# A one-column carry copy in an attention kernel, issued by ScalarE instead of VectorE

## The reference, cut to what matters

```python
def _time_mix_layer(x, ln_w, ln_b, Wk, Wv, Wr, Wo):
    normed = _layer_norm(x, ln_w, ln_b)
    k = jnp.einsum('btd,ed->bte', normed, Wk)
    v = jnp.einsum('btd,ed->bte', normed, Wv)
    r = jax.nn.sigmoid(jnp.einsum('btd,ed->bte', normed, Wr))
    kv = k * v
    def step(state, kv_t):
        state = DECAY * state + (1.0 - DECAY) * kv_t
        return (state, state)
    _, states = jax.lax.scan(step, init, jnp.swapaxes(kv, 0, 1))
    y = r * jnp.swapaxes(states, 0, 1)
    return x + jnp.einsum('btd,ed->bte', y, Wo)
```

## Time and profile before

| | us |
|---|---|
| median of 3 runs | 1204.03 |
| lowest and highest of them | 1203.22, 1205.99 |
| span of the profiled execution, first to last instruction | 1212.0 |
| own time of the profiled execution | not given beside its span |
| busy in the span: PE, DVE, ACT, POOL | 1091.2, 909.5, 614.8, 652.6 |

### The profile page before, as it was taken

The page is one execution under the profiler, slowest core; times in us unless marked ns, Lnnn a source line. Parts: engine busy times, 40 slices in busy tenths (PEclk is TensorE's granted clock), DMA queues, the critical chain, the costliest instruction groups (busy, mean ns, idle before and its releaser), DMA issues. The chain is left out here.

```text
span 1212.0 us, 22064 instructions
## 1 busy us (share of the span) xinstructions
PE 1091.2 (90%) x6624; PEld 957.5 (79%) x6624; DVE 909.5 (75%) x2050; ACT 614.8 (51%) x1019; POOL 652.6 (54%) x560
## 2 busy tenths in 40 slices
PE   6999999999999998757999999999999999999900
PEld 6778887777777786646888888888888999999900
DVE  5788888888888887744776766777776778888737
ACT  3345444444444444333444555555555666666528
POOL 1011554444444544665667667666573777777534
PEclk9899999999999998859999999999999999999965
DMA  4011221111121121356566657878775888998569
GB/s 157 18 53 52 53 54 53 53 52 52 52 52 52 52 53 36 76 138 180 127 150 168 158 126 168 207 200 210 182 202 156 196 248 243 241 221 246 112 190 383
DMA packets 80243, 164.34 MB, mean 136 GB/s; under 512 B 27568, under 2 KB 44976, under 8 KB 79920
## 3 DMA queue, kind: packets, MB, share of 16 engines
q1 hardware_dynamic: 49968, 127.72, 33.4%
q0 software_dynamic: 30208, 35.81, 16.8%
HBM read 118.78 MB, written 44.70 MB: 135 GB/s over the span
## 5 line engine op out<-in xcount | busy, mean ns | idle before, releaser
L1181 POOL DMA_INDIRECT x_acc<-fy_sb,pair_out x136 | 254.2, 1869 | 133.8 <-issue 56.0
L1371 PE MATMUL fring<-fxh,fw_hi 128*128 128x256 f32 (+1 forms) x704 | 236.0, 335 | 11.7 <-issue 8.0
L1373 PE MATMUL fring<-fxh,fw_lo 128*128 128x256 f32 (+1 forms) x704 | 234.2, 333 | 0.0
L1372 PE MATMUL fring<-fxl,fw_hi 128*128 128x256 f32 (+1 forms) x704 | 233.9, 332 | 0.0
L1201 ACT ACTIVATE fw_hi<-w_raw 128x1024 fp32r<-128x1024 f32 x156 | 163.4, 1054 | 107.9 <-PE fy L1416 90.1
L1263 DVE TENSOR_TENSOR fw_lo<-w_raw,fw_hi 128x1024 fp32r<-128x1024 f32 x156 | 189.6, 1219 | 15.5 <-ACT fw_hi L1201 12.4
L98 POOL DMA_INDIRECT xg<-x_src,pair_in x136 | 147.9, 1088 | 85.2 <-issue 43.6
L546 POOL TENSOR_TENSOR rs<-ve,neg_half 128x4 f32<-128x4 f32 x48 | 55.6, 1159 | 254.6 <-DVE nm L633 254.5
L88 POOL DMA_INDIRECT slot_list<-pairs,slot_u x128 | 144.5, 1129 | 50.3 <-issue 35.6
L870 PE MATMUL ring<-xh,w_hi 128*128 128x512 f32 x384 | 160.7, 418 | 2.1 <-issue 2.0
L1414 PE MATMUL fy<-fw_hi,gh 128*128 128x256 f32 x544 | 155.8, 286 | 0.0
(11 more groups left out here) (149 smaller groups left out, 2013.1 us busy)
## 6 DMA issues: line engine op xcount, KB each, us to landing
w_raw<-w_ffn SPq DMA_DIRECT2D x156, 512.0 KB
x_in<-h SPq DMA_DIRECT2D x16, 512.0 KB
x_src<-x SPq DMA_DIRECT2D x16, 512.0 KB
x_acc<-x SPq DMA_DIRECT2D x16, 512.0 KB
acc<-x_acc SPq DMA_DIRECT2D x16, 512.0 KB, 7.1
out<-o SPq DMA_DIRECT2D x16, 512.0 KB, 6.2
xg<-x_src,pair_in POOLq DMA_INDIRECT x136
x_acc<-fy_sb,pair_out POOLq DMA_INDIRECT x136
```

Source lines behind the costliest of these rows:

```text
L1181: nc.gpsimd.indirect_dma_start(x_acc, bass.IndirectOffsetOnAxis(pair_out[j][:, q, 0:1].bitcast(U32), 0), y[j][:, q, :], None, compute_op=A ...
L1371: nc.tensor.matmul(out, hi, rows_hi, start=dc == 0, stop=False)
L1372: nc.tensor.matmul(out, hi, rows_lo, start=False, stop=False)
L1373: last = nc.tensor.matmul(out, lo, rows_hi, start=False, stop=dc == DC - 1)
```

## The change

The carry copy of `recur` leaves VectorE's stream. A new function of ScalarE, `carry_on`, does the same copy as an activation with function Copy. For layer 1 it is issued in front of `keep_k` of e=1 (for e=0) and behind `x_hi(1, s-1)` (for e=1); for layer 2 behind `keep_k` of e=1 (for e=0) and at the end of ScalarE's step (for e=1). It is left out for chunk 15. The scan now waits until the carry of the chunk before it, same e, has been copied, since `state` is overwritten.

```diff
+            def carry_on(l, n, e):
+
+                if within(n, 0, CHUNKS - 2):
+                    act.wait_ge(s_sn[l], n * 2 + e + 1)
+                    nc.scalar.activation(carry[:, l, e, bass.ds(n + B, 1)], state[l][:, e, CH - 1:CH],
+                                         ACT.Copy).then_inc(s_cy[l], 1)
+
...
                             normalize(1, xr, normed[1], s - 1, s_n[1])
+                        if e == 1:
+                            carry_on(0, s, 0)
                         if at(s, 0):
                             keep_k(0, s, e, j, None, 0)
...
                 if layer2:
                     x_hi(1, s - 1)
+                if layer1:
+                    carry_on(0, s, 1)
                 if at(s, CHUNKS):
                     normalize3(s, half, j)
...
                         keep_k(1, s - 1, 1, j, s_kv[0], s * 2 + 2)
+                    carry_on(1, s - 1, 0)
...
                 if layer2:
                     gate_r(1, s - 1, 1, j)
+                    carry_on(1, s - 1, 1)
...
                 if within(n, 1, CHUNKS):
                     dve.wait_ge(s_y[l], n * 2 + e - 1)
-                dve.wait_ge(s_cy[l], n * 2 + 2)
+                if within(n, 1, CHUNKS):
+                    dve.wait_ge(s_cy[l], n * 2 + e + 1)
+                else:
+                    dve.wait_ge(s_cy[l], 2)
                 nc.vector.tensor_tensor_scan(state[l][:, e, :], decay[:, :], kv[:, e, :],
                                              carry[:, l, e, bass.ds(n, 1)], ALU.mult, ALU.add).then_inc(s_sn[l], 1)
-                dve.wait_ge(s_sn[l], n * 2 + e + 1)
-                nc.vector.tensor_copy(carry[:, l, e, bass.ds(n + B, 1)], state[l][:, e, CH - 1:CH]).then_inc(s_cy[l], 1)
```

## The result

The changed kernel takes 1188.75 us (median of 4 runs, 1186.91 to 1190.67) against 1203.72 us (4 runs) before: 15.0 us less, a ratio of 0.9871, 95% interval 0.9845 to 0.9898. It is faster, as forecast, and by more: the forecast was 1192.5 and the range began at 1189.0, 0.25 us above what came.

A forecast was written before the change was run, and what follows sets the result against it. One 30.12 us loop through VectorE, GpSimd, ScalarE and TensorE, none full, was the bound. Step savings summed to 11.6 us, span 1212.0 to 1200.4, less 8.0 for the median: forecast 1192.5 us, range 1189 to 1199 (8 in 10).

The forecast's parts named there:

- ScalarE's price of 0.10: ScalarE's layer 1, e=0 copy between normalizing activations and keep_k: costs the loop 0.10 us per step, bounds 0 and 0.36.
- the second reading: Odd step before took 0.45 us longer through 0.44 us idle VectorE ahead of xr, so VectorE time returns one to one.
- start, to the gate copy of step 3: Attention's first steps: start and end together save 0 to 0.2 us.
- steps 3, 4, 14: Written-out attention steps: 0.47 us each from three copies of 0.19 less 0.10, taken as 1.2 us for TensorE's little waiting.
- steps 5, 13: Attention steps half in and half out of the loop: save 0.9 us each, 1.8 us together.
- even steps 6, 8, 10, 12: Even loop steps: each saves 0.36 + 0.41 + 0.30 - 0.10 = 0.97 us, 3.9 us together.
- odd steps 7, 9, 11: Odd loop steps, with the iteration's end: each saves 0.36 + 0.82 + 0.36 - 0.10 = 1.44 us, 4.3 us together.
- step 15: Attention step behind the written-out step 14: both layer-2 copies save 0.4 us.
- A: VectorE's issue time moves to the next instruction, each copy gives back only 0.19 us; 1198 us; chance 0.15.
- B: TensorE becomes the bound, or the later part gives some back; 1191 to 1196 us; chance 0.13 beyond the forecast's own bounds.
- C: Nothing arrives: some wait put down as slack binds in each step; 1203 to 1205 us; chance 0.05.
- D: Slower: ScalarE's copy ahead of keep_k costs over about 1.1 us per step, as with table loads (1206.6 us); chance 0.07.

The follow-up runs named there:

- wait_back: Changed kernel with VectorE again waiting for the scan's semaphore right behind each scan, without a copy of its own; median 1199.1 us, ratio to before 0.9959.
- defer: Kernel before, all four copies still on VectorE but each issued one or two operations later; median 1191.1 us, ratio to before 0.9901.
- before_again: Kernel before, unchanged, profiled once more; 1206.3 us (1 run), profile span 1204.4 us.
- unroll_before: Kernel before with all 20 steps written out, no hardware loop; median 1196.8 us, ratio to before 0.9880.
- after_again: Changed kernel, unchanged, timed and profiled again; median 1197.5 us, ratio to before 0.9892.
- unroll_after: Changed kernel with all 20 steps written out, no hardware loop; median 1186.2 us, ratio to before 0.9813.
- three: Changed kernel with the layer 1, e=0 copy put back on VectorE, the other three on ScalarE; median 1191.6 us, ratio to before 0.9913.
- act_twice: Changed kernel with one more one-column ScalarE activation in front of the layer 1, e=0 copy; median 1195.3 us, ratio to before 0.9860.

## Why the prediction was right and where it was not

**Right: the loop, the places and the mechanism.** The four engines are one loop; time off VectorE in it comes back one to one; three of four copies count; a copy costs much more than its 0.15 us. wait_back shows that the wait is what costs, defer that the engine hardly matters, the two written-out kernels that the iteration's end and the loop's addresses were part of it. ScalarE's price of 0.10 was 0.09. An even step was to save 0.97 and saves 0.91 (30.12 to 29.21). That is what its parts give: the gate copy to the end of the layer-2 statistics is 0.70 shorter in step 10, `kv` to `xl` 0.29 shorter, `normed` to `keep_k` 0.08 longer.
The Trainium skill ("ScalarE: Activation LUTs", Rules for kernel authors) has about 0.3 us for an activation whose bias is a pointer operand. The copy here has no bias, so that figure was not its price, though the prediction took it for every activation. The rows here give 0.20 from start to end and 0.09 from start to start.

**Right by luck: the second reading.** "Its one difference" between the odd and the even step before was said to be the 0.44 us ahead of `xr`, and that number met the 0.45 us between the steps. The rows say otherwise. The last operation of the layer-2 statistics (`nm`), and the activations that wait for it through GpSimd, in step 9 and in step 10:

```profile
301.93 0.16 DVE L633 TENSOR_SCALAR nm<-mv 128x4 f32<-128x4 f32 x1
305.02 2.08 ACT L407 ACTIVATE normed<-xr,nb,rs 128x256 f32<-128x256 f32 x4 [2.92 <-POOL nb L548]
...
332.30 0.16 DVE L633 TENSOR_SCALAR nm<-mv 128x4 f32<-128x4 f32 x1
335.21 2.08 ACT L407 ACTIVATE normed<-xr,nb,rs 128x256 f32<-128x256 f32 x4 [2.32 <-POOL nb L548]
```

From the gate copy to `nm` the odd step took 13.83 us and the even one 13.63, only 0.20 apart, since the even step has delays of its own (the 0.30 ahead of the scan at 321.98 among them). From `nm` to `normed`, GpSimd's part, it was 3.09 against 2.91, 0.18 apart. The remaining 0.07 lies behind. That is also why the steps did not come out alike, as the prediction wanted them, but the odd ones shorter: without the 0.44 the even step's own delays are left.

**Wrong: the size.** The mechanism was right, and what failed was the sum. It gave 11.6 us; the same terms came to 14.5 at step 18, by the differences of the two first profiles. The odd steps are the term that was too small by most (4.3 against 5.1), then the written-out steps, step 15 and the start:

| term of the sum | said | measured |
|---|---|---|
| start, to the gate copy of step 3 | 0 to 0.2 for start and end | 0.57 |
| steps 3, 4, 14 | 1.2 | 1.81 |
| steps 5, 13 | 1.8 | 1.99 |
| even steps 6, 8, 10, 12 | 3.9 | 3.71 |
| odd steps 7, 9, 11 | 4.3 | 5.10 |
| step 15 | 0.4 | 0.99 |
| step 16 | in "start and end" | 0.33 |

The start's 0.57 is 0.97 less 0.40: the first `kv` starts at 22.90 after and at 23.30 before, ahead of any carry, and before_again has it at 23.08, so that is scatter of the first loads. The 0.57 itself is rough. From the first `kv` to the gate copy of step 3 the three kernels with copies behind the scans (before, before_again, unroll_before) take 85.97 to 86.57 us, and the changed one, after_again and unroll_after 85.40 to 85.86: about 0.5 us on average for the copies of steps 0 to 2, which the sum had put at next to nothing. The 0.33 of step 16 is not the change's: before_again takes 18.01 us there, as the changed kernel does.

*The odd steps.* The sum had 1.44 us for one; step 9 saved 1.70 (30.57 to 28.87). I took the two copies in front of the statistics at 0.36 + 0.82 and the last one at 0.36. The gate copy to `nm` came out 1.26 us shorter (13.83 to 12.57), 0.08 more than that, and `kv` to `xl` 0.35. The rest of the 1.70 lies in handoffs that I held constant: from `nm` to `normed` it takes 0.09 less (3.09 to 3.00), `kv` starts 0.03 instead of 0.10 behind the end of `keep_k`, and `xl` to the gate copy takes 0.02 less; ScalarE's copy takes 0.09 off again. Each is read from the two profiles; why they shrank is not shown.

*The written-out steps.* "TensorE has only 0.21 us of waiting left, so I take 1.2 for the three" read the room too small. TensorE's waits in steps 3 and 14 before, beside the 0.21 of step 4:

```profile
131.47 1.07 PE L828 MATMUL tp<-ident,x 128*128 128x128 f32 x8 [0.59 <-DVE xl L638]
...
461.18 1.06 PE L828 MATMUL tp<-ident,x 128*128 128x128 f32 x8 [0.43 <-DVE xl L638]
```

Steps 3, 4 and 14 saved 0.78, 0.41 and 0.62, each 0.19 or 0.20 more than TensorE's recorded wait in it. A matmul's recorded end lies behind the start of the next (in step 4 one of 0.40 us starts at 161.41 and the next at 161.65), so a recorded idle time is too short: a full step of TensorE is 28.41 us, as unroll_after shows, not 28.6. Since these steps became TensorE's, they gave back its whole wait, and not the three copies' 0.47.

*Step 15 and 16.* VectorE's part of step 15 fell as said (the statistics end 11.29 us behind the gate copy against 11.60). The rest is TensorE's clock. Busy time of PE, PEld, DVE, ACT and POOL, then the granted clock, of step 15 in before, changed and three, each in a fence of its own:

```profile
468.20:491.86 23.66, 18.74 (x94) 15.40 (x94) 17.05 (x58) 6.87 (x14) 7.80 (x9) 0.86 0.20 46
```

```profile
454.60:477.29 22.69, 18.09 (x94) 14.88 (x94) 16.83 (x55) 7.12 (x16) 7.63 (x9) 0.92 0.21 48
```

```profile
453.94:477.46 23.52, 18.92 (x94) 15.55 (x94) 16.81 (x55) 7.10 (x16) 7.60 (x9) 0.85 0.20 46
```

For the same 94 matmuls the granted clock of the step was 0.86 before, 0.92 after and 0.85 in three: behind TensorE's wait for `y` in this step (4.09, 3.65 and 3.67 us) part of the work ran at the lower level, 1.2 GHz, a longer part in the first and the last. With a mean of 0.85 or 0.86 the step takes 23.5 to 24.0 us (before_again, act_twice and unroll_after too), with 0.92 it takes 22.7 (after_again too). From the end of the statistics to the gate copy the changed kernel needs 11.39 us and three 12.24, with the same work. That is the 0.8 us that three loses against the changed kernel, and about 0.7 of the 0.99 that the change gains in this step. Which of the two a kernel meets I could not steer. The prediction had named the clock, but only for the stretch behind the attention.

**From step 18 to the median.** The gain at the experts' start is 14.25 us (530.98 to 516.73), the medians differ by 15.0, in the second comparison by 13.0 (0.9892). The parts behind the attention scatter by several us in both kernels, so nothing more can be ascribed to the change. The forecast of 1192.5 misses by 3.75 us: as the first profiles divide it, 2.9 in the terms above and 0.4 in the first loads; 0.3 more is that the kernel before has a median of 1203.72 here and had 1204.03 in the prediction; the rest is scatter. The range was missed by less than two comparisons of the same two kernels differ: the ratio 0.9892 of the second would put the changed kernel at 1190.7, inside it.

**The rivals.** A (issue time stays exposed) falls: no gap is left behind any scan. B falls in the loop, where TensorE still waits up to 0.5 us. In the written-out steps TensorE is the bound now, yet they gain more than the sum had, not less. C and D fall; there is no new table load.

## What to carry to other kernels

A tiny operation that depends on the long one just ahead of it in the same stream can cost much more than it lasts: here a copy of 0.15 us cost about 0.19 in written-out code, 0.3 to 0.4 in the hardware loop and 0.82 as the last work of its body. Price it from the long operation's end to the next start, and add the 0.08 us by which an independent operation starts before that end. Before moving it to another engine, try moving it one or two operations later in its own stream: here that brought 11.3 of 12.0 us. Look first at the last instruction of a hardware loop's body: here the iteration's end hid under the scan only when nothing waited behind it. And see whether the loop can be written out: here that alone gave the kernel before 11.4 us.

## What was not expected

- The waits alone, one behind each scan and with nothing behind them but independent work, made the loop's steps 0.6 (even) and 1.2 us (odd) longer (wait_back).
- The hardware loop itself cost this kernel 11.4 us over steps 3 to 14 with the copies behind the scans (329.88 against 318.44), and 4.7 us without them (317.98 against 313.24).
- Behind a wait of TensorE of 3.65 us in one kernel and 3.67 in another the mean granted clock of the step was 0.92 and 0.85, which moves the result by 0.8 us.
